# State-space stage: half-length folded frequency convolution, fused state products, and the sum of two planes on TensorE

## Chip, cores and metric

One core of a Trainium2 chip. The metric is the device time of one execution in microseconds, here the median of three runs.

## The reference, cut to what matters

Six blocks follow one another on x (8 sequences, 256 tokens, 128 channels): feed-forward, attention, feed-forward, mixture of experts, state-space, mixture of experts. The change is in the state-space block, and it prepares weights in the attention block.

```python
xz = einsum('bld,ed->bel', layernorm(x), in_proj_w)       # 512 rows: x and z, 256 channels each
out   = mamba_branch(xz, ...)                             # for each of 16 states: h = dA * h + dBu; y = sum(h * C)
out_b = mamba_branch(xz[:, :, ::-1], ...)                 # the same backwards, with weights of its own
x, z = split(xz, 2, axis=1)
xf = fftn(x, axes=(-2, -1))                               # over 256 channels and 256 tokens
xc = concatenate([xf.real, xf.imag], axis=1)              # 512 channels
xc = silu(conv(xc, fft_conv_w, width 5, padding 2) + fft_conv_b)
re, im = split(xc, 2, axis=1)
v = abs(ifftn(re + 1j * im, axes=(-2, -1)) * max(silu(z)))
y = out + out_b[:, :, ::-1] + normalized(v)
x = x + einsum('bdl,od->blo', y, out_proj_w)
```

All of it is f32. Since x is real, its transform is symmetric: the value at (-channel, -token) is the conjugate of that at (channel, token).

## The kernel before

Each block is a phase with its own tiles, semaphores and instruction streams, and a barrier stands between phases. `mamba_phase` (from L1349) runs its eight sequences in a pipeline written out by hand: `mamba_schedule` (L1315) calls `step(f, m, o)` of each engine, where f is the sequence whose inputs are made, m the one that is scanned, and o the one that is finished. A step has eight slots (UNITS), and each slot scans one unit of m: one direction and four of the 16 states, for two halves of 128 channels (DC = 2). All waits are semaphores, and every engine works its stream in order.

In a unit TensorE spreads four rows of B and of C over the partitions into PSUM (`spread`, L1524); ScalarE makes the decays (`decay`, L1678); VectorE multiplies B with dx for each half (L1811), scans each half (L1818) and multiplies each half with C (L1823); GpSimd adds four planes to two (L1940) and two to one (`halve`, L1943); TensorE sums that plane into y in PSUM (`total`, L1536), two slots later. h has three buffers (HBUFS), so VectorE's unit n waits for the sum of unit n - 3.

The frequency path of m runs beside that on TensorE in pieces: token transform (slot 0, L1469), ScalarE's copy (L1687), channel transform (L1478), ScalarE's copies into `fc` (L1691), the convolution over 4 input and 4 output blocks and 5 taps, 80 f32 products of 256 columns in slots 1 to 5 (L1489, PIECES), SiLU on ScalarE from PSUM (L1697, slot 5), and the inverse transforms in slots 6 and 7 (L1499, L1508). An f32 product is two records in the trace. In slot 6 `project_out` (L1561) follows these on TensorE, and VectorE's `add_output` (L1883) waits for it.

GpSimd also splits B and C into bf16 parts in slots 4 and 6 (`parts`, L1957 to L1963) and fetches the next sequence's input in slot 4 (`fetch`, L1949). VectorE ends a step with `steps` (L1784, L1789) and begins the next with `energy` (L1828); between the units lie small instructions for o (L1833, L1836, L1843, L1851, L1877).

In `attn_phase` (from L764) a step handles one sequence and four heads. There GpSimd rotates (L993, L995) and normalizes (L1002), and TensorE transposes what that leaves (L841). SP's queue is empty in that phase; the state-space weights (`cw`, 5 MB, among them) are loaded in the phase before the state-space one.

Of the kernel before, what the change touches and what calls it, by code (L numbers as in the profile page):

```python
# [763 lines left out]
def attn_phase(k, a):  # L764
# [3 lines left out]
    with ExitStack() as ctx:  # L768
# [11 lines left out]
        stx = k.sb("at_stx", [P, 2, 2, 6], ctx)  # L780
        sc = [k.psum(f"at_sc{h}", [P, 2, N], ctx) for h in range(4)]
# [4 lines left out]
                 "pr_sb", "rinv_sb", "pn01_sb", "pn23_sb", "tp_ps", "pt_sb", "cx_ps", "cx_sb", "op_ps", "x_sb"]  # L786
# [200 lines left out]
        def _(pool):  # L987
# [17 lines left out]

            for step in steps:
# [300 lines left out]

# [41 lines left out]
def mamba_phase(k, w):  # L1349
# [4 lines left out]
    winr, gw = w.winr, w.gm[:, 0, :, :]  # L1354
    dd = w.gm[:, 1, :, :].rearrange("p t n -> p (t n)")[:, 0:2 * DC * P].rearrange("p (r c n) -> p r c n", r=2, c=DC)
    with ExitStack() as ctx:
# [31 lines left out]
        f_bank = [k.psum(f"mb_f{i}", [P, 512], ctx) for i in range(2)]  # L1388
# [6 lines left out]
                 "b_ps", "c_ps", "da_sb", "dbu_sb", "scan_sb", "hc_sb", "half_sb", "hs_sb", "y_ps", "ym_sb", "dd_sb", "dd_ps",  # L1395
# [19 lines left out]
        def _(pe):  # L1415
# [44 lines left out]
            def frequency(m, slot, half):  # L1460
# [3 lines left out]
                if slot == 0 and half == 1:  # L1464
                    if m.b == 0:
                        pe.wait_ge(s["gw_sb"], 2)
# [15 lines left out]
                elif slot in (1, 2, 3, 4, 5) and (slot > 1 or half == 1):  # L1482
# [9 lines left out]
                    if slot == 5 and half:  # L1492
                        last.then_inc(s["f_ps"], 1)
# [603 lines left out]
```

## Time and profile before

| | us |
|---|---|
| median of 3 runs (2118.87 to 2120.63) | 2119.89 |
| the profiled execution | 2119.23 |
| its span, first to last instruction | 2117.40 |
| TensorE busy | 1961.0 (93%) |
| VectorE busy | 1683.6 (80%) |
| ScalarE busy | 1313.8 (62%) |
| GpSimd busy | 1170.4 (55%) |

The profile calls TensorE PE (PEld its weight loads), VectorE DVE, ScalarE ACT, GpSimd POOL and SyncE SP. The shares are means over six blocks, so windows are read by stage: attention lies at about 490 to 805 us, the state-space stage at about 1327 to 2047 us, its first scanned sequence from 1360 us. Busy time counts overlapping instructions of an engine once. "[1.60 <-PE ps_mb_w L1561]" behind a row means that its engine was idle for 1.60 us before it, until that instruction released it.

### The profile page before, as it was taken

Reading aid. Unit: us, or ns where it says so; the run is one execution under the profiler, and the core shown is the slowest. Engines: PE = TensorE matmul, PEld = TensorE weight load, DVE = VectorE, ACT = ScalarE, POOL = GpSimd, SP = SyncE. Lnnn points to the kernel's source line nnn. Section 1 sums busy time; section 2 is a strip of 40 time slices with the busy share of each in tenths; the row PEclk is TensorE's granted clock in tenths of the full one; section 3 lists DMA queues with packets and bytes.
Section 4 is the critical chain, followed back from the end, with each engine's and each line's share of the span. In section 5 each row is a group of like instructions: output and inputs, shape, how many; then the busy total and the mean of one; then the engine's idle time right before and its main releaser. Section 6 shows DMA issues by size and latency. Waiting matters only on the chain. (4 is left out here: it accounts for less than half of the span.)

```text
span 2117.4 us, 39266 instructions
## 1 busy us (share of the span) xinstructions
PE 1961.0 (93%) x14044; PEld 1440.9 (68%) x14044; DVE 1683.6 (80%) x2822; ACT 1313.8 (62%) x2591; POOL 1170.4 (55%) x1605
## 2 busy tenths in 40 slices
PE   6999999968999995999999869799999999999978
PEld 5677776646888873677777636587787777877745
DVE  5877777766888875777777766599999999999974
ACT  1566666644777772766666543558577576685543
POOL 2666666615667765666667503264755646646323
PEclk9999999988999996999999979899999999999989
DMA  4666666620000003665666423000000000000000
GB/s 136 159 158 158 159 159 158 149 65 1 2 1 2 2 1 94 156 163 155 162 155 161 124 69 140 1 1 1 1 1 1 1 1 1 1 1 1 1 16 21
DMA packets 147745, 144.86 MB, mean 68 GB/s; under 512 B 14048, under 2 KB 106976, under 8 KB 146912
## 3 DMA queue, kind: packets, MB, share of 16 engines
q1 hardware_dynamic: 127968, 132.91, 23.2%
q10 hardware_dynamic: 19584, 9.44, 2.5%
q8 instruction: 113, 1.85, 0.4%
q14 instruction: 80, 0.66, 0.1%
HBM read 94.07 MB, written 38.80 MB: 63 GB/s over the span
## 5 line engine op out<-in xcount | busy, mean ns | idle before, releaser
L577 DVE TENSOR_REDUCE sb_f_mx<-ps_f_s 128x2 f32<-128x512 f32 x768 | 501.9, 677 | 189.4 <-PE ps_f_s L354 186.3
L507 ACT ACTIVATE sb_f_pt<-ps_f_t 128x1024 f32<-128x1024 f32 x384 | 383.4, 1023 | 164.6 <-PE ps_f_t L371 162.4
L1940 POOL TENSOR_TENSOR sb_mb_h<-sb_mb_h 128x512 f32<-128x512 f32 x128 | 165.0, 1311 | 303.4 <-DVE sb_mb_h L1823 302.3
L354 PE MATMUL ps_f_s<-sb_f_stack 96*128 96x256 bf16 x1536 | 302.2, 279 | 27.8 <-DMA sb_f_stack<-f_scr 13.9
L1818 DVE TENSOR_TENSOR_SCAN sb_mb_h<-sb_mb_da,sb_mb_h 128x1024 f32<-128x1024 f32 x128 | 304.3, 2416 | 2.7 <-ACT sb_mb_da L1678 2.7
L1489 PE MATMUL ps_mb_f<-sb_mb_fc,sb_mb_cw 128*128 128x256 f32 x1280 | 286.8, 381 | 6.7 <-ACT sb_mb_fc L1691 6.6
L1489 PEld LDWEIGHTS ps_mb_f<-sb_mb_fc,sb_mb_cw 128*128 128x128 f32 x1280 | 239.7, 190 | 41.4 <-ACT sb_mb_fc L1691 8.9
L371 PE MATMUL ps_f_t<-sb_f_stack 128*128 128x256 bf16 x1536 | 232.1, 273 | 9.0 <-DMA sb_f_stack<-sb_f_mrow 5.3
L1678 ACT ACTIVATE sb_mb_da<-sb_mb_dl,sb_mb_an 128x255 f32<-128x255 f32 x512 | 211.0, 495 | 31.2 <-DVE sb_mb_h L1818 30.6
L354 PEld LDWEIGHTS ps_f_s<-sb_f_stack 96*128 96x128 bf16 x1536 | 131.8, 99 | 129.1 <-issue 44.0
L428 PE MATMUL ps_f_a<-sb_f_pt,sb_f_v 128*32 128x256 f32 x3072 | 189.1, 387 | 0.0
L371 PEld LDWEIGHTS ps_f_t<-sb_f_stack 128*128 128x128 bf16 x1536 | 146.5, 97 | 37.4 <-DMA sb_f_stack<-sb_f_mrow 12.4
L1811 DVE TENSOR_TENSOR sb_mb_h<-ps_mb_b,sb_mb_dx 128x1024 f32<-128x1024 f32 x128 | 149.9, 1210 | 10.3 <-PE ps_mb_b L1524 10.3
L1823 DVE TENSOR_TENSOR sb_mb_h<-sb_mb_h,ps_mb_c 128x1024 f32<-128x1024 f32 x128 | 148.6, 1200 | 1.6 <-PE ps_mb_c L1524 1.6
L1002 POOL TENSOR_SCALAR sb_at_pr<-sb_at_pr,sb_at_rinv 128x256 f32<-128x256 f32 x128 | 116.1, 927 | 60.8 <-DVE sb_at_rinv L925 60.8
L669 POOL TENSOR_SCALAR sb_f_nmx<-sb_f_mx 128x16 f32<-128x16 f32 x96 | 36.5, 380 | 188.8 <-DVE sb_f_mx L577 188.8
L428 PEld LDWEIGHTS ps_f_a<-sb_f_pt,sb_f_v 128*32 128x32 f32 x3072 | 91.3, 111 | 72.6 <-issue 24.5
L1042 ACT ACTIVATE sb_at_pr<-ps_at_sc,sb_at_nmx 128x256 f32<-128x256 f32 x256 | 118.9, 492 | 5.9 <-DVE sb_at_nmx L919 3.4
L1943 POOL TENSOR_TENSOR sb_mb_h<-sb_mb_h 128x256 f32<-128x256 f32 x128 | 118.6, 948 | 0.0
L690 POOL TENSOR_TENSOR sb_f_r<-sb_f_qf,sb_f_parts 128x512 f32<-128x512 f32 x96 | 113.9, 1186 | 7.7
L695 POOL TENSOR_TENSOR sb_f_parts<-sb_f_r,sb_f_parts 128x512 bf16<-128x512 f32 x96 | 111.7, 1163 | 7.7
L1027 ACT ACTIVATE sb_at_pt<-ps_at_tp 128x512 f32<-128x512 f32 x128 | 69.9, 604 | 66.0 <-PE ps_at_tp L841 66.0
(248 smaller groups left out, 3998.2 us busy)
## 6 DMA issues: line engine op xcount, KB each, us to landing
f_scr<-sb_f_parts SPq DMA_DIRECT2D x96, 384.0 KB, 2.8
sb_f_stack<-f_scr SPq DMA_DIRECT2D x192, 192.0 KB, 3.1
sb_f_stack<-f_scr SPq DMA_DIRECT2D x192, 128.0 KB, 3.2
sb_f_stack<-f_scr SPq DMA_DIRECT2D x192, 64.0 KB, 3.3
sb_f_stack<-sb_f_mrow ACTq DMA_DIRECT2D x96, 96.0 KB
sb_mb_cw<-in_cw SPq DMA_DIRECT2D x1, 5120.0 KB, 19.8
sb_prep_wn<-in_wn SPq DMA_DIRECT2D x6, 512.0 KB, 7.3
sb_m_w<-in_w SPq DMA_DIRECT2D x6, 256.0 KB, 3.3
```

What stands on the lines that cost most here:

```text
L354: last = nc.tensor.matmul(s_bank[j % 2][:, h, :], stack[0:ROWS, a.n % STACKS, 0, g * GROUP + pair * 2 + h, half * P:(half + 1) * P], stack ...
L371: last = nc.tensor.matmul(t_bank[i % 2][:, h, :], stack[:, e.n % STACKS, 1, g * GROUP + h, half * P:(half + 1) * P], stack[:, e.n % STACKS ...
L428: last = nc.tensor.matmul(act_bank[h * SLOT:(h + 1) * SLOT, g * N:(g + 1) * N], v[:, u.two, half, h * NG + g, :], pt[:, u.two, g, half, h, ...
L507: nc.scalar.activation(pt[:, e.two, g, half, :, :], t_bank[i % 2][:, :, :], ACT.Exp).then_inc(s["pt_sb"], 1)
L577: nc.vector.tensor_reduce(mx[:, a.two, half, head:head + 2], s_bank[j % 2][:, :, :], AX.X, ALU.max)\
L1042: last = nc.scalar.activation(pr[:, m.two, i, :], sc[h][:, i % 2, :], ACT.Exp, scale=scale, bias=nmx[:, m.two, i:i + 1], accum_out=rsum[:, ...
L1489: last = nc.tensor.matmul(f_bank[(1 + oc // 2) % 2][:, (oc % 2) * N:(oc % 2 + 1) * N], cw[:, ic, tap, oc * P:(oc + 1) * P], fc[:, ic, tap: ...
L1678: last = nc.scalar.activation(da[:, un % 2, c, i, 1:N], dl[:, m.parity, r, c, 1:N], ACT.Exp, scale=an[:, r, c, n:n + 1])
L1811: nc.vector.tensor_tensor(hb[:, c, :, :], b_bank[:, :, :], dx[:, m.parity, r, c:c + 1, :].broadcast_to([P, SG, N]), ALU.mult)\
L1818: nc.vector.tensor_tensor_scan(flat, da[:, un % 2, c, :, :].rearrange("p i n -> p (i n)"), flat, 0.0, ALU.mult, ALU.add).then_inc(s["scan_ ...
L1823: nc.vector.tensor_tensor(hb[:, c, :, :], hb[:, c, :, :], c_bank[:, :, :], ALU.mult).then_inc(s["hc_sb"], 1)
L1940: nc.gpsimd.tensor_tensor(hb[:, c, 0:2, :], hb[:, c, 0:2, :], hb[:, c, 2:4, :], ALU.add).then_inc(s["half_sb"], 1)
```

## The change

- The convolution is computed on half the tokens. The even and the odd part of the spectrum are kept (`even`, `odd`), GpSimd makes eight sums and differences of neighbours (`neighbours`, 2 x 128 to 131 elements each), and TensorE multiplies ten folded inputs (FOLDS) by ten folded weights: 10 x 2 x 4 f32 products of 128 to 131 columns, in slots 1 to 4. VectorE unfolds the two halves (`unfold`, two instructions, after the scans of unit 5), ScalarE's SiLU then works in place in SBUF at the start of slot 6 (`gate_frequency`).
- The folded weights are made in the attention phase: `cwa` and `cwb` are loaded (10 MB), GpSimd combines them (38 additions of 128x512), SP stores them to `cw_scr`, from where `cw` is loaded.
- Both channel halves go through one instruction for the product with B, and one for that with C; the scans stay two.
- GpSimd's second halving goes; TensorE sums two planes into y instead of one.
- The transforms before the convolution shrink to what the symmetry leaves; PIECES has seven pieces; some calls in TensorE's slots change places.

```diff
-PIECES = (0, 10, 19, 28, 37, 46, 54, 62, 71, 80)
+PIECES = (0, 11, 21, 32, 44, 57, 68, 80)
+FOLDS = ((658, 129, 0), (789, 128, 128), (264, 130, 0), ...
 attn_phase, SP
+            for i in range(2 * DC):
+                sp.dma_start(wa[:, p, c, :, :], d["cwa"][:, p, c, :, :]).then_inc(raw[i], 16)
+                sp.dma_start(wb[:, p, c, :, :], d["cwb"][:, p, c, :, :]).then_inc(raw[i], 16)
+            for a in range(1, len(FOLDS)):
+                sp.wait_ge(s["wfold_sb"], 2 * a)
+                sp.dma_start(d["cw"][:, a, :, :], wf[:, a, :, :]).then_inc(s["w_stored"], 16)
+            sp.wait_ge(s["w_stored"], 16 * len(FOLDS))
 attn_phase, GpSimd, after rotate(f, 1)
+                for i in range(joined(step), joined(step + 1)):
+                    combine(i)
 mamba_phase, TensorE: frequency
-                        last = nc.tensor.matmul(f_bank[(1 + oc // 2) % 2][:, (oc % 2) * N:(oc % 2 + 1) * N],
-                                                cw[:, ic, tap, oc * P:(oc + 1) * P], fc[:, ic, tap:tap + N],
+                        if a >= 2 and n == 0:
+                            pe.wait_ge(s["fold_sb"], m.b * (len(FOLDS) - 2) + a - 1)
+                        last = nc.tensor.matmul(f_both[:, oc // 2, oc % 2 * N + to:oc % 2 * N + to + cols],
+                                                cw[:, a, ic, oc * P:(oc + 1) * P], fold[:, ic, at:at + cols],
 total
-                last = nc.tensor.matmul(y_bank[:, c, ::1 - 2 * r], k.ident[:, :], h[:, n % HBUFS, c, 0, :],
+                for i in range(SG // 2):
+                    last = nc.tensor.matmul(y_bank[:, c, ::1 - 2 * r], k.ident[:, :], h[:, n % HBUFS, c, i, :],
 ScalarE
+            def gate_frequency(m):
+                act.wait_ge(s["split_sb"], m.b + 1)
+                for oc in range(XC_CH):
+                    last = nc.scalar.activation(fs[:, oc, :], fs[:, oc, :], ACT.Silu, bias=cb[:, oc:oc + 1])
 VectorE: scan
-                for c in range(DC):
-                    nc.vector.tensor_tensor(hb[:, c, :, :], b_bank[:, :, :],
-                                            dx[:, m.parity, r, c:c + 1, :].broadcast_to([P, SG, N]), ALU.mult)\
+                nc.vector.tensor_tensor(hb, both(b_bank), dx[:, m.parity, r, :, :].rearrange("p c (o n) -> p c o n", o=1)
+                                        .broadcast_to([P, DC, SG, N]), ALU.mult).then_inc(s["dbu_sb"], 1)
                 dve.wait_ge(s["da_sb"], n)
+                dve.wait_ge(s["dbu_sb"], n)
                 for c in range(DC):
...
+                if un == 5:
+                    unfold(m)
                 dve.wait_ge(s["c_ps"], n)
+                dve.wait_ge(s["scan_sb"], DC * n)
+                nc.vector.tensor_tensor(hb, hb, both(c_bank), ALU.mult).then_inc(s["hc_sb"], 1)
+            def unfold(m):
+                dve.wait_ge(s["f_sb"], FREQ * m.b + 4)
+                half = f_split[:, :, :, HALF_N - 1:0:-1]
+                nc.vector.tensor_tensor(fs4[:, :, :, 1:HALF_N], half, diff, ALU.add)
+                nc.vector.tensor_tensor(fs4[:, :, :, N - 1:HALF_N:-1], half, diff, ALU.subtract).then_inc(s["split_sb"], 1)
 GpSimd: halve, step
+                pool.wait_ge(s["hc_sb"], n)
                 for c in range(DC):
                     nc.gpsimd.tensor_tensor(hb[:, c, 0:2, :], hb[:, c, 0:2, :], hb[:, c, 2:4, :], ALU.add).then_inc(s["half_sb"], 1)
-                for c in range(DC):
-                    nc.gpsimd.tensor_tensor(hb[:, c, 0, :], hb[:, c, 0, :], hb[:, c, 1, :], ALU.add).then_inc(s["hs_sb"], 1)
+                    if m and un in (1, 2, 3):
+                        for a in range(3 * un - 1, min(3 * un + 2, len(FOLDS))):
+                            neighbours(m, a)
                     if m:
                         halve(m, un)
```

## Rows read from the trace of the kernel before

**Rows 1.** Windows; us, busy of PE, PEld, DVE, ACT, POOL, clock, DMA share, GB/s

```profile
600.00:700.00 100.00, 100.00 (x910) 81.14 (x904) 81.96 (x197) 75.19 (x241) 69.73 (x88) 1.00 0.01 2
1610.00:1690.00 80.00, 78.89 (x366) 61.75 (x366) 78.23 (x64) 54.15 (x108) 48.55 (x40) 1.00 0.00 1
1960.00:1970.00 10.00, 7.13 (x28) 5.35 (x28) 9.96 (x9) 7.57 (x15) 3.61 (x4) 0.83 0.01 2
```

**Rows 2.** Waits of DVE, 1449 to 1960 us: us in total, times, longest

```profile
DVE sb_x L1883 <- PE ps_mb_w L1561: 10.2, 6, 2.2
```

**Rows 3.** Timeline of DVE, one sequence: start us, us, engine line op

```profile
1713.06 0.67 DVE L1833 TENSOR_REDUCE sb_mb_zm<-sb_mb_sz 128x2 f32<-128x512 f32 x1
1713.77 0.84 DVE L1836 SCALAR_TENSOR_TENSOR sb_mb_zo<-sb_mb_zm 128x2 f32<-128x2 f32 x1
1714.53 2.34 DVE L1811 TENSOR_TENSOR sb_mb_h<-ps_mb_b,sb_mb_dx 128x1024 f32<-128x1024 f32 x2
1716.80 4.46 DVE L1818 TENSOR_TENSOR_SCAN sb_mb_h<-sb_mb_da,sb_mb_h 128x1024 f32<-128x1024 f32 x2
1721.18 2.32 DVE L1823 TENSOR_TENSOR sb_mb_h<-sb_mb_h,ps_mb_c 128x1024 f32<-128x1024 f32 x2
...
1724.08 0.67 DVE L1851 TENSOR_TENSOR sb_mb_ys<-ps_mb_y,sb_mb_sz 128x512 f32<-128x512 f32 x1
...
1736.23 4.70 DVE L1818 TENSOR_TENSOR_SCAN sb_mb_h<-sb_mb_da,sb_mb_h 128x1024 f32<-128x1024 f32 x2
...
1746.14 5.08 DVE L1818 TENSOR_TENSOR_SCAN sb_mb_h<-sb_mb_da,sb_mb_h 128x1024 f32<-128x1024 f32 x2
...
1755.65 5.05 DVE L1818 TENSOR_TENSOR_SCAN sb_mb_h<-sb_mb_da,sb_mb_h 128x1024 f32<-128x1024 f32 x2
...
1765.13 5.40 DVE L1818 TENSOR_TENSOR_SCAN sb_mb_h<-sb_mb_da,sb_mb_h 128x1024 f32<-128x1024 f32 x2
```

**Rows 4.** Timeline of POOL, the same sequence

```profile
1712.09 2.50 POOL L1940 TENSOR_TENSOR sb_mb_h<-sb_mb_h 128x512 f32<-128x512 f32 x2 [8.39 <-DVE sb_mb_h L1823]
1714.55 1.42 POOL L1943 TENSOR_TENSOR sb_mb_h<-sb_mb_h 128x256 f32<-128x256 f32 x2
...
1755.16 3.39 POOL L1943 TENSOR_TENSOR sb_mb_h<-sb_mb_h 128x256 f32<-128x256 f32 x2
```

**Rows 5.** Groups by line and form, PE: count, busy us, mean ns, idle before

```profile
L1489 PE MATMUL ps_mb_f<-sb_mb_fc,sb_mb_cw 128*128 128x256 f32 x1280 | 286.8, 381 | 6.7 <-ACT sb_mb_fc L1691 6.6
...
L1536 PE MATMUL ps_mb_y<-sb_mb_h,sb_ident 128*128 128x256 f32 x256 | 66.1, 381 | 3.3 <-POOL sb_mb_h L1943 3.3
...
L867 PE MATMUL ps_at_vc<-sb_at_wo,sb_at_cx 128*128 128x128 f32 x256 | 33.9, 275 | 0.7 <-ACT sb_at_cx L1034 0.7
...
L1478 PE MATMUL ps_mb_f<-sb_mb_yk,sb_mb_gm 128*128 128x256 f32 x128 | 30.9, 396 | 3.6 <-ACT sb_mb_yk L1687 3.6
```

**Rows 6.** Timeline of DVE, first scanned sequence, three waits

```profile
1374.66 4.47 DVE L1818 TENSOR_TENSOR_SCAN sb_mb_h<-sb_mb_da,sb_mb_h 128x1024 f32<-128x1024 f32 x2 [2.68 <-ACT sb_mb_da L1678]
...
1421.02 2.35 DVE L1823 TENSOR_TENSOR sb_mb_h<-sb_mb_h,ps_mb_c 128x1024 f32<-128x1024 f32 x2 [1.31 <-PE ps_mb_c L1524]
...
1435.68 2.35 DVE L1811 TENSOR_TENSOR sb_mb_h<-ps_mb_b,sb_mb_dx 128x1024 f32<-128x1024 f32 x2 [2.48 <-PE ps_mb_b L1524]
```

**Rows 7.** Timeline of ACT, the sequence of rows 3

```profile
1715.46 1.06 ACT L1691 ACTIVATE sb_mb_fc<-ps_mb_f 128x512 f32<-128x512 f32 x2
```

**Rows 8.** Timeline of POOL, attention, a middle step and the last

```profile
654.40 3.63 POOL L1002 TENSOR_SCALAR sb_at_pr<-sb_at_pr,sb_at_rinv 128x256 f32<-128x256 f32 x4 [1.72 <-DVE sb_at_rinv L925]
...
791.71 3.62 POOL L1002 TENSOR_SCALAR sb_at_pr<-sb_at_pr,sb_at_rinv 128x256 f32<-128x256 f32 x4 [5.10 <-DVE sb_at_rinv L925]
```

**Rows 9.** DMA issues: out<-in, queue, count, KB each, median us to landing

```profile
f_scr<-sb_f_parts SPq DMA_DIRECT2D x96, 384.0 KB, 2.8
```

**Rows 10.** Timeline, end of attention

```profile
802.67 0.42 DVE L944 TENSOR_TENSOR sb_x<-sb_x,ps_at_vc 128x256 f32<-128x256 f32 x1 [8.71 <-PE ps_at_vc L867]
```

**Rows 11.** One line's instructions, PEld: ns min/median/max, first and last start

```profile
L867 PEld LDWEIGHTS ps_at_vc<-sb_at_wo,sb_at_cx x256: 186/192/192, 518.8 to 802.2; 128*128 128x128 f32 x128
```

More of the change, by code:

```diff
@@ L1472, in frequency @@
                     pe.wait_ge(s["f_sb"], seen + 1)
[L1473 to L1482 removed]
+                    for part, cols in enumerate((slice(0, EVEN_COLS), slice(EVEN_COLS, EVEN_COLS + ODD_COLS))):
+                        n = cols.stop - cols.start
+                        for mc in range(DC):
+                            last = nc.tensor.matmul(f_bank[part][:, mc * n:(mc + 1) * n], gw[:, mc * P:(mc + 1) * P], yt[:, cols],
+                                                    start=True, stop=True)
+                        last.then_inc(s["f_ps"], 1)
+                elif slot in (1, 2, 3, 4) and (slot > 1 or half == 1):
                     piece = 2 * slot + half - 3
@@ L1502, in frequency @@
                         last.then_inc(s["f_ps"], 1)
-                elif slot == 7 and half == 1:
-                    pe.wait_ge(s["f_sb"], seen + 5)
-                    for dc in range(DC):
-                        for c in range(XC_CH):
-                            ri, kc = divmod(c, 2)
-                            last = nc.tensor.matmul(f_bank[(1 + dc) % 2][:, :],
-                                                    uk[:, kc, ri * CH_I + dc * P:ri * CH_I + (dc + 1) * P], gi[:, c, :],
-                                                    start=c == 0, stop=c == XC_CH - 1)
-                    last.then_inc(s["f_ps"], 1)
+                elif slot == 7:
+                    dc = half
+                    if dc == 0:
+                        pe.wait_ge(s["f_sb"], seen + 6)
+                    for c in range(XC_CH):
+                        ri, kc = divmod(c, 2)
+                        last = nc.tensor.matmul(f_bank[dc], uk[:, kc, ri * CH_I + dc * P:ri * CH_I + (dc + 1) * P], gi[:, c, :],
+                                                start=c == 0, stop=c == XC_CH - 1)
+                    if dc == 1:
+                        last.then_inc(s["f_ps"], 1)
             def spread(m, un, which):
@@ L1521, in spread @@
                     pe.wait_ge(s["bc_sb"], 2 * m.b + 2)
-                since(pe, read, DC * (m.b * UNITS + un))
+                since(pe, read, m.b * UNITS + un)
                 for i in range(SG):
@@ L1565, in combine @@
             def combine():
-                for part in range(2):
-                    cols = w.gm[:, :, 0:2, :] if part == 0 else w.gm[:, :, 2:3, :]
-                    for c in range(DC):
-                        last = nc.tensor.matmul(f_bank[part][:, 0:(2 - part) * CH_I], winr[:, c, :],
-                                                cols[:, c, :, :].rearrange("p t n -> p (t n)"), start=c == 0, stop=c == DC - 1)
+                for c in range(DC):
+                    last = nc.tensor.matmul(f_bank[0][:, 0:CH_I], winr[:, c, :], w.gm[:, c, :], start=c == 0, stop=c == DC - 1)
                 last.then_inc(s["gw_ps"], 1)
@@ L1721, in step @@
                 for slot in range(UNITS):
+                    if m and slot == 6:
+                        gate_frequency(m)
                     if f and 2 <= slot <= 6:
```

260 lines of the change are left out of this document (167 added, 93 removed).

## The prediction

> **What bounds the kernel now.** I read the windows by stage first. In the attention stage TensorE is busy 100 of 100 us, with VectorE at 82 and GpSimd at 70; in the state-space stage TensorE is busy 78.9 and VectorE 78.2 of 80 us [rows 1]. So the stage that the change rewrites has two full engines, and taking work from one of them is worth only what the other waits for it. The waits give that figure: in six whole sequences (1449 to 1960 us) VectorE waited 10.2 us, always in front of the same instruction, the output addition of L1883, which waits for TensorE: 1.7 us a sequence [rows 2]. With six sequences in 511 us, one takes about 85 us, and VectorE's own instructions are some 83 of it.
>
> The timeline of VectorE in one sequence shows of what they are made [rows 3]. A unit (there are eight) is two products with B, two scans, two products with C. In unit 1: products 1714.53 to 1716.80 (2.27 us), scans to 1721.18 (4.38), products of 2.32 us, of which 2.24 count, since the next instruction overlaps them. Instructions that don't need the one just before start some 0.07 us before it ends (1714.53 + 2.34 is 1716.87, the first scan, which needs only the first product, starts at 1716.80). One that needs it starts 0.04 us after its end (L1833 ends at 1713.06 + 0.67 = 1713.73, L1836 starts at 1713.77).
>
> A third thing is in these rows: the same two scans take 4.46 us in unit 1, but 4.70, 5.08, 5.05 and 5.40 in units 3 to 6, 2.39 us more in a sequence. GpSimd's timeline says why [rows 4]: the second halving takes 1.42 us for its two instructions when no scan runs, and 3.39 us in unit 5, where it meets the scans. VectorE instructions with two SBUF inputs and GpSimd get in each other's way. The products read PSUM and don't: the pair at 1714.53 and the second halving at 1714.55 ran side by side, with 2.34 and 1.42 us.
>
> **TensorE's part, costed from the rows by form [rows 5].** The convolution is 1280 records of 256 columns, 286.8 us, 224 ns each; the folded one has as many, of 128 to 131 columns. L867 has f32 records of 128 columns: 33.9 us for 256, 132 ns each. So 1280 x 132 = 169 us, 118 less. The channel transform (L1478) goes from 128 records of 256 columns to 64 of about 131: 30.9 to 8.4 us, 22 less. The sum into y gets 256 records more (L1536: 66.1 us for 256, of which I count all). Net 118 + 22 - 66 = 74 us, 9 us a sequence. None of that is on the path beyond the waits of [rows 2], and in the first sequence 1.31 and 2.48 us for TensorE and 2.68 us for ScalarE [rows 6], of which I give the change half, since the chain ahead of it gets a shorter set-up product. Of the 1.7 us I take back 1.1: the output projection still stands behind the eight wide products of slot 6, and these now wait for SiLU, which has been moved behind VectorE's unfolding; and TensorE will stand idle for some us before slot 6. Where it was idle for 2.9 of 10 us, the granted clock was 0.83 on average, part of it at the lower of its two levels (1.2 instead of 2.4 GHz) [rows 1]. The ends are 0 and 1.7.
>
> **VectorE's part, a sequence.** Fusing: one product of 2048 elements. 512 elements take 0.67 us (L1851), 1024 take 1.21 (two overlapped in 2.34), so 2048 take 2.29. The scan now needs the whole product just ahead of it: 2.29 + 0.04 against 2.27, +0.06. The second product needs the scan just ahead: 4.46 + 0.04 against 4.38, +0.12. The second product itself is 2.22 against 2.24. That is +0.16 a unit, 1.28 for eight, less 0.12 in unit 5, where the unfolding stands between: **+1.15**. (If a dependent start cost nothing, -0.55: the lower end. The upper is the sum.)
>
> Unfolding: two additions of 508 elements, one input in PSUM. L1851 has that size: 0.67 us, less the overlap of 0.07 [rows 3], twice: **+1.2**. No row reads PSUM backwards in VectorE; the slowest form here, the scan, takes about twice as long per element as a product, so 2.4 is the upper end, 1.2 the lower; I take the row of the same size.
>
> GpSimd against the scans: the second halving goes, but the first one now starts only when the whole fused product has ended (before, after its first half), runs 2.50 us [rows 4], and the next scan starts about 2.25 us after that end. So units 5 and 6 still meet it (0.25), and the B/C split (unit 4 and 6) and the fetch (unit 5) stay: I leave 0.6, 0.7 and 0.65 in units 4 to 6 and nothing in unit 3: 1.95 of the 2.39, -0.45. New are the eight neighbour additions of 258 elements with two SBUF inputs, in slots 1 to 3, each ahead of that slot's halving on GpSimd's queue. What waits behind them is the halving and, behind it, TensorE's sum, which VectorE needs only three units later; so the queue costs nothing, and the meeting with the scans does. The first three come when ScalarE has written the spectrum, which in this trace ends at 1715.46 + 1.06 = 1716.52 [rows 7], just ahead of the scans of unit 1 at 1716.80; the others follow the halvings of units 1 and 2. One instruction that gets between two scans costs about 0.5 (unit 5: 5.05 against 4.46), so 0.5 in each of three units and 0.25 for one that holds up the start in unit 2: 1.75. Together **+1.3**. Ends: -2.4 (no excess left and no meeting) and 8 x 0.59 - 0.45 = +4.3.
>
> Sum for a sequence: 1.15 + 1.2 + 1.3 - 1.1 = +2.55. Seven sequences so (the last counted like the six in the middle): +17.9. The first: 3.65 - 1.31 - 2.48 - 1.34 = -1.5.
>
> **Attention.** GpSimd gets 38 additions of 128x512, about 1.25 us each (the first halving has that size), one or two a step. Its free time ahead of L1002 is 1.72 us a step [rows 8], so one fits. Behind it on the queue stands L1002, whose result TensorE wants. Steps with two additions (five of 33) can stall TensorE for part of a microsecond: 0.8 in all. At the end five additions follow the last L1002 (791.71 + 3.62 = 795.33, so 801.6), then a store of 512 KB; one of 384 KB took 2.8 us [rows 9], so it lands at about 805, and VectorE's last addition of the stage ended at 803.1 [rows 10], with statistics behind it: 1.2. Together **+2**, ends 0 and 16 (0.5 in every step). The 10.5 MB loaded here and the 5 MB stored run on SP's queue, which has no other work in this stage; the first addition is due four steps in. The load of cw in the MoE stage has the size that it had.
>
> Sum: 17.9 - 1.5 + 2 = +18.4 on the profiled execution of 2119.2 us (span 2117.4), 2137.6; the median of the runs, 2119.9, lies 0.7 above it: **2138**.
>
> **A rule that says otherwise.** The rows show the 0.07 us overlap and the 0.04 us gap above [rows 3]. The Trainium skill (VectorE: DVE Perf Modes, "The DRAIN you can't avoid") says that the next instruction starts only when the pipe is empty, semaphore or not, and that fewer instructions is what counts. By that fusing would be the gain of rival 2; the rows speak against it.
>
> **Rivals.**
> 1. *GpSimd gets out of the way* (faster). The additions fall beside products, and with the second halving the excess goes: contention -2.4 instead of +1.3. A sequence is then 1.15 + 1.2 - 2.4 - 1.1 = -1.15, seven -8; the first -5.2; attention +2: **2109**. It decides once contention falls by more than 1.25 us a sequence. For it: the halving stands in the longest stretch of contention [rows 4]. Against it: scans are half of VectorE's time, and the B/C split stays.
> 2. *Dependent starts cost nothing*: fusing is then 2.29 - 0.07 = 2.22 us for each product in place of 2.27 and 2.24, -0.55 in eight units. A sequence +0.85, seven +6, the first -3.2, attention +2: **2125**.
> 3. *Weight loads bound the short products* (the change doesn't do what it says): the loads beside L867 last 192 ns [rows 11], and if the pace were 190 ns a record, the convolution would save 44 us and the transform 19, less than the 66 added. The waits for TensorE stay: eight sequences x 3.65 + 2 = +31: **2151**. L867's 132 ns speak against it.
> 4. *Attention pays*: 0.5 us in each of 33 steps, +16 instead of +2: **2152**. For it: TensorE is 100% busy there. Against it: 1.72 us of slack.
>
> **Chances.** Forecast 0.50 (its own range 2126 to 2150, from the ends of unfolding and contention taken in part), rival 1 0.18, rival 2 0.14, rival 3 0.06, rival 4 0.12. A measurement of this kernel can tell about 0.2% (4 us) from no change. Faster: rival 1 and the low end of rival 2, 0.20. The same: most of rival 2 and the low edge of the forecast, 0.14. Slower: the rest, 0.66. The range 2110 to 2152 leaves out half of rival 1 and the upper tails of 3 and 4.
>
> **What would show it.** Right: VectorE over 97% busy in the state-space stage and TensorE near 88%; a sequence of 87 us; records of the convolution near 132 ns; each scan pair of units 1 to 3 longer than 4.46 us; fused products near 2.29 us, the scan 0.04 us behind them. Wrong: scan pairs at 4.46 in units 1 to 3 (rival 1), no gap behind a product (rival 2), records near 190 ns (rival 3), TensorE under 98% in attention (rival 4).

## The result and the profile after

The changed kernel took 2141.74 us (median of four executions, 2137.34 to 2144.62), the kernel before 2120.26 beside it: a ratio of 1.0101, 95% interval 1.0082 to 1.0119. The profiled execution took 2142.74 us, its span is 2140.9, 23.5 us above the 2117.4 of before. Beside the experiments the kernel before had medians of 2115.2 to 2116.2, so kernels are compared below by their ratios, and by what one sequence takes in their traces. One execution of e6 below (2134.72 us, granted clock 0.91) was in a slower state of the chip and is left out of its ratio.

The windows by stage of the changed kernel (columns as in [rows 1]), and one whole sequence, from one output addition of VectorE to the next:

```profile
600.00:700.00 100.00, 99.55 (x900) 81.46 (x896) 83.91 (x197) 74.70 (x238) 83.88 (x99) 1.00 0.02 7
...
1610.00:1690.00 80.00, 68.01 (x378) 54.54 (x377) 78.37 (x49) 55.49 (x111) 37.48 (x29) 0.94 0.00 1
...
1785.50:1874.33 88.83, 75.50 (x409) 58.76 (x408) 85.39 (x53) 58.80 (x116) 44.27 (x34) 0.94 0.00 1
```

The same for a sequence of the kernel before:

```profile
1689.61:1774.37 84.76, 83.66 (x385) 64.94 (x384) 82.99 (x66) 58.44 (x112) 49.68 (x42) 1.00 0.00 1
```

TensorE lost 8 us of work in a sequence and the sequence grew by 4. The waits, first of VectorE and then of TensorE, in five sequences of the changed kernel (1520 to 1963 us), show who waits now:

```profile
DVE sb_x L1967 <- PE ps_mb_w L1627: 6.9, 6, 1.6
...
PE ps_mb_c L1588 <- DVE sb_mb_h L1900: 53.8, 28, 4.3
```

TensorE waits 53.8 us for VectorE, while VectorE's old wait, the one of [rows 2], is still there. VectorE's timeline of one sequence answers to [rows 3]; the numbering of the units is the same (unit 0 starts at 1800.25):

```profile
1800.25 2.28 DVE L1888 TENSOR_TENSOR sb_mb_h<-ps_mb_b,sb_mb_dx 128x2048 f32<-128x2048 f32 x1
1802.63 4.47 DVE L1894 TENSOR_TENSOR_SCAN sb_mb_h<-sb_mb_da,sb_mb_h 128x1024 f32<-128x1024 f32 x2
1807.21 2.29 DVE L1900 TENSOR_TENSOR sb_mb_h<-sb_mb_h,ps_mb_c 128x2048 f32<-128x2048 f32 x1
...
1813.17 5.27 DVE L1894 TENSOR_TENSOR_SCAN sb_mb_h<-sb_mb_da,sb_mb_h 128x1024 f32<-128x1024 f32 x2
...
1824.52 4.96 DVE L1894 TENSOR_TENSOR_SCAN sb_mb_h<-sb_mb_da,sb_mb_h 128x1024 f32<-128x1024 f32 x2
...
1831.98 1.25 DVE L1953 SCALAR_TENSOR_TENSOR sb_mb_nm<-sb_mb_mv,sb_mb_rs 128x2 f32<-128x2 f32 x1
...
1835.54 4.47 DVE L1894 TENSOR_TENSOR_SCAN sb_mb_h<-sb_mb_da,sb_mb_h 128x1024 f32<-128x1024 f32 x2
...
1859.68 0.66 DVE L1906 TENSOR_TENSOR sb_mb_yk<-ps_mb_f,sb_mb_fold 128x508 f32<-128x508 f32 x1
1860.26 0.67 DVE L1907 TENSOR_TENSOR sb_mb_yk<-ps_mb_f,sb_mb_fold 128x508 f32<-128x508 f32 x1
1860.85 2.27 DVE L1900 TENSOR_TENSOR sb_mb_h<-sb_mb_h,ps_mb_c 128x2048 f32<-128x2048 f32 x1
...
1865.42 5.05 DVE L1894 TENSOR_TENSOR_SCAN sb_mb_h<-sb_mb_da,sb_mb_h 128x1024 f32<-128x1024 f32 x2
```

Three things are to be seen. A scan starts 0.10 us after the end of the product that it needs (1800.25 + 2.28 = 1802.53, next start 1802.63), the product with C 0.11 us after the scans. Scan pairs of 4.47 us stand beside pairs of up to 5.27. And L1953, a product of two elements a partition, takes 1.25 us. GpSimd's timeline at the places of the last two and at the end of slot 5, which answers to [rows 4]:

```profile
1813.12 5.74 POOL L2053 TENSOR_TENSOR sb_mb_fold<-sb_mb_fold 128x260 f32<-128x260 f32 x3 [1.03 <-ACT sb_mb_fold L1757]
...
1831.95 2.51 POOL L2027 TENSOR_TENSOR sb_mb_h<-sb_mb_h 128x512 f32<-128x512 f32 x2 [6.80 <-DVE sb_mb_h L1900]
...
1863.20 2.50 POOL L2027 TENSOR_TENSOR sb_mb_h<-sb_mb_h 128x512 f32<-128x512 f32 x2 [5.59 <-DVE sb_mb_h L1900]
1865.66 2.67 POOL L2068 TENSOR_TENSOR sb_mb_bcf<-sb_mb_bcf,sb_mb_bc 128x256 f32<-128x256 f32 x1
```

The neighbour additions meet the scans at 1813.17. The halving that starts at 1831.95 holds the tiny product at 1831.98. The halving at 1863.20 starts when the whole fused product has ended and still runs when the next scans start, at 1865.42; the first addition of the B/C split (L2068) stands behind it and takes 2.67 us beside them.

TensorE at the end of slot 5 and in slot 6, where VectorE's wait comes from:

```profile
1863.18 1.03 PE L1588 MATMUL ps_mb_c<-sb_mb_bc,sb_mb_sel 128*128 128x256 bf16 x4 [4.28 <-DVE sb_mb_h L1900]
1864.00 5.52 PE L1562 MATMUL ps_mb_f<-sb_mb_gi,sb_mb_yk 128*128 128x512 f32 x8
...
1869.80 3.60 PE L1562 MATMUL ps_mb_f<-sb_mb_gi,sb_mb_yk 128*128 128x512 f32 x8
1873.23 1.05 PE L1627 MATMUL ps_mb_w<-sb_mb_wop,sb_mb_ys 128*128 128x128 f32 x8
```

After 4.28 idle us the first eight wide records take 5.52 us, the next eight 3.60. The projection stands behind all of them. The windows there have granted clocks of 0.80 and 0.86, so part of either is at the lower level, 1.2 GHz:

```profile
1855.00:1865.00 10.00, 5.72 (x27) 4.13 (x26) 10.00 (x6) 6.32 (x13) 4.41 (x4) 0.80 0.00 1
1865.00:1875.00 10.00, 10.00 (x33) 5.27 (x32) 8.33 (x6) 4.56 (x11) 8.65 (x7) 0.86 0.00 0
```

The groups of the new records, to be read beside [rows 5]:

```profile
L1601 PE MATMUL ps_mb_y<-sb_mb_h,sb_ident 128*128 128x256 f32 x512 | 133.8, 409 | 6.5 <-POOL sb_mb_h L2027 6.5
...
L1551 PE MATMUL ps_mb_f<-sb_mb_fold,sb_mb_cw 128*128 128x129 f32 x512 | 63.8, 279 | 0.1
```

The four forms of L1551 have 160.2 us for 1280 records, 125 ns each, with 192 ns weight loads beside them.

In attention, VectorE's last addition and the first instruction of the next block that waits for the barrier; first the changed kernel, then the kernel before, whose first row is in [rows 10]:

```profile
802.74 0.42 DVE L989 TENSOR_TENSOR sb_x<-sb_x,ps_at_vc 128x256 f32<-128x256 f32 x1 [7.11 <-PE ps_at_vc L912]
...
808.87 0.25 DVE L92 RECIPROCAL sb_rs<-sb_sd 128x16 f32<-128x16 f32 x1 [4.97 <-ACT sb_sd L86]
```

```profile
806.70 0.25 DVE L92 RECIPROCAL sb_rs<-sb_sd 128x16 f32<-128x16 f32 x1 [2.88 <-ACT sb_sd L86]
```

The added 23.5 us lie here: up to the first product with B 2.5 (1362.51 against 1360.03); from there to the first output addition, over two sequences, -2.4 (157.63 against 160.05); five middle sequences +19.1 (88.58 each, against 84.77); the rest to the last output addition +4.0; behind it +0.3.

### The profile page after: what moved, and what is told of

It is laid out like the page before. It is cut to its first block and busy times, and to the rows that moved or that the text cites. A ratio compares the mean times of both kernels' runs of the same rounds, so it can differ in the third digit from the quotient of the medians.

```text
span 2140.9 us, 39573 instructions
## 1 busy us (share of the span) xinstructions
PE 1894.6 (88%) x14232; PEld 1396.3 (65%) x14232; DVE 1709.5 (80%) x2713; ACT 1317.7 (62%) x2622; POOL 1180.8 (55%) x1579
## 5 line engine op out<-in xcount | busy, mean ns | idle before, releaser
L2027 POOL TENSOR_TENSOR sb_mb_h<-sb_mb_h 128x512 f32<-128x512 f32 x128 | 173.3, 1375 | 345.0 <-DVE sb_mb_h L1900 345.0
L371 PE MATMUL ps_f_t<-sb_f_stack 128*128 128x256 bf16 x1536 | 232.0, 273 | 11.5 <-DMA sb_f_stack<-sb_f_mrow 7.7
L1888 DVE TENSOR_TENSOR sb_mb_h<-ps_mb_b,sb_mb_dx 128x2048 f32<-128x2048 f32 x64 | 145.8, 2278 | 7.2 <-PE ps_mb_b L1588 7.2
L1900 DVE TENSOR_TENSOR sb_mb_h<-sb_mb_h,ps_mb_c 128x2048 f32<-128x2048 f32 x64 | 146.3, 2286 | 5.8
L1551 PE MATMUL ps_mb_f<-sb_mb_fold,sb_mb_cw 128*128 128x129 f32 (+3 forms) x1280 | 149.9, 276 | 1.2 <-POOL sb_mb_fold L2053 1.1
L1551 PEld LDWEIGHTS ps_mb_f<-sb_mb_fold,sb_mb_cw 128*128 128x128 f32 x1280 | 147.0, 193 | 2.0 <-POOL sb_mb_fold L2053 1.2
L1601 PE MATMUL ps_mb_y<-sb_mb_h,sb_ident 128*128 128x256 f32 x512 | 133.8, 409 | 6.5 <-POOL sb_mb_h L2027 6.5
L1601 PEld LDWEIGHTS ps_mb_y<-sb_mb_h,sb_ident 128*128 128x128 f32 x512 | 100.7, 206 | 26.1 <-POOL sb_mb_h L2027 8.7
```

What stands on the lines that cost most here:

```text
L371: last = nc.tensor.matmul(t_bank[i % 2][:, h, :], stack[:, e.n % STACKS, 1, g * GROUP + h, half * P:(half + 1) * P], stack[:, e.n % STACKS ...
L1551: last = nc.tensor.matmul(f_both[:, oc // 2, oc % 2 * N + to:oc % 2 * N + to + cols], cw[:, a, ic, oc * P:(oc + 1) * P], fold[:, ic, at:at ...
L1601: last = nc.tensor.matmul(y_bank[:, c, ::1 - 2 * r], k.ident[:, :], h[:, n % HBUFS, c, i, :], start=un == 0 and c == 0 and i == 0, stop=un ...
L1888: nc.vector.tensor_tensor(hb, both(b_bank), dx[:, m.parity, r, :, :].rearrange("p c (o n) -> p c o n", o=1) .broadcast_to([P, DC, SG, N]), ...
L1900: nc.vector.tensor_tensor(hb, hb, both(c_bank), ALU.mult).then_inc(s["hc_sb"], 1)
L2027: nc.gpsimd.tensor_tensor(hb[:, c, 0:2, :], hb[:, c, 0:2, :], hb[:, c, 2:4, :], ALU.add).then_inc(s["half_sb"], 1)
```

## The experiments

The table has every kernel. "Period" is a fifth of the time between the starts of two output additions five sequences apart. "Work" is the time of VectorE's instructions in it, each counted from its start to the start of the next, so that overlaps and small gaps are in it; what is left is waits. "Scans" is the scans' part of the work. Without contention the scans take 8 x 4.38 = 35.0 us where the product with C starts half by half (the overlap makes 4.38 of 4.46), and 36.5 to 36.6 where it needs both scans; what lies above is called their excess. The rest of the work is products with B and C (36.12 before, 36.76 changed, 36.23 in e1), unfolding (1.17 where there is one) and small instructions (9.53, 10.32 and 8.79). Each trace is of one execution, and those of e3, e4 and e6 are of their shortest or second shortest (2123.18 us where the median is 2132.40, 2128.79 where it is 2132.32, 2095.43 where it is 2108.25): the gains that their periods show are larger than those of their ratios. The diffs are shortened: the waits that change with an edit are left out, but for GpSimd's in e1.

| kernel | ratio to before, 95% | period | work | waits | scans |
|---|---|---|---|---|---|
| before | 1 | 84.77 | 83.10 | 1.67 | 37.45 |
| changed | 1.0101 (1.0082 to 1.0119) | 88.58 | 87.28 | 1.30 | 39.03 |
| e1, products per half | 1.0008 (0.9998 to 1.0018) | 85.32 | 82.17 | 3.15 | 35.98 |
| e2, output first | 1.0099 (1.0084 to 1.0114) | 87.56 | 86.77 | 0.79 | 38.65 |
| e3, no neighbours | 1.0078 (1.0065 to 1.0090) | 86.88 | 86.00 | 0.88 | 37.77 |
| e4, tiny instructions | 1.0068 (1.0056 to 1.0079) | 86.80 | 85.93 | 0.87 | 39.33 |
| e5 = e1 + e2 + e4 | 0.9964 (0.9952 to 0.9976) | 84.11 | 81.30 | 2.81 | 35.96 |
| e6 = e5, unfolding early | 0.9948 (0.9927 to 0.9969) | 82.15 | 81.17 | 0.98 | 35.89 |
| e7, only B fused | 1.0018 (1.0007 to 1.0030) | 85.47 | 83.23 | 2.24 | 36.40 |
| e8, before + fused products | 1.0109 (1.0093 to 1.0125) | 87.47 | 87.47 | 0.00 | 39.91 |
| e9, before + e2 + e4 | 1.0004 (0.9991 to 1.0018) | 85.08 | 82.30 | 2.78 | 37.30 |
| e10 = e1 + second halving | 1.0072 (1.0054 to 1.0089) | 86.86 | 86.05 | 0.81 | 39.17 |

**e1: products per half.**

```diff
-                nc.vector.tensor_tensor(hb, both(b_bank), dx[...both halves...], ALU.mult).then_inc(s["dbu_sb"], 1)
+                for c in range(DC):
+                    nc.vector.tensor_tensor(hb[:, c], b_bank, dx[...half c...], ALU.mult).then_inc(s["dbu_sb"], 1)
-                nc.vector.tensor_tensor(hb, hb, both(c_bank), ALU.mult).then_inc(s["hc_sb"], 1)
+                for c in range(DC):
+                    dve.wait_ge(s["scan_sb"], DC * (n - 1) + c + 1)
+                    nc.vector.tensor_tensor(hb[:, c], hb[:, c], c_bank, ALU.mult).then_inc(s["hc_sb"], 1)
 GpSimd: halve
-                pool.wait_ge(s["hc_sb"], n)
                 for c in range(DC):
+                    pool.wait_ge(s["hc_sb"], DC * (n - 1) + c + 1)
```

> Changed kernel with both products split per channel half again (32 instructions a sequence in place of 16, the waits counted per half), everything else as in the changed kernel. Theory: what fusing costs is the dependent start; an instruction that needs the one just ahead starts 0.10 us after its end, one that doesn't starts 0.07 us before it. A unit without contention then goes from 9.17 to 8.89 us, 2.1 us a sequence, eight sequences 17 us: 2125 us, a sequence near 86.5 in place of 88.6. Rival A (the size in the prediction, a gap of 0.04): 1.15 a sequence, 2132 us. Rival B (a dependent start costs nothing, fewer instructions win): 0.55 a sequence the other way, 2146 us.

The gain is larger than the theory's: work falls by 5.1 us, and 1.9 us of that come back as waits. VectorE's groups in five sequences of e1, and the same two of the changed kernel:

```profile
L1896 DVE TENSOR_TENSOR_SCAN sb_mb_h<-sb_mb_da,sb_mb_h 128x1024 f32<-128x1024 f32 x80 | 183.1, 2328 | 4.5 <-ACT sb_mb_da L1739 4.5
...
L1956 DVE SCALAR_TENSOR_TENSOR sb_mb_nm<-sb_mb_mv,sb_mb_rs 128x2 f32<-128x2 f32 x5 | 0.8, 160 | 0.2
```

```profile
L1894 DVE TENSOR_TENSOR_SCAN sb_mb_h<-sb_mb_da,sb_mb_h 128x1024 f32<-128x1024 f32 x80 | 191.9, 2439 | 4.1
...
L1953 DVE SCALAR_TENSOR_TENSOR sb_mb_nm<-sb_mb_mv,sb_mb_rs 128x2 f32<-128x2 f32 x5 | 6.3, 1258 | 0.2
```

The dependent starts are the part foreseen: products 36.76 to 36.23, and 1.42 in the scans (36.46 without contention, where the unfolding parts unit 5, to 35.04); 1.95 together. The other 3.2 are meetings with GpSimd: the scans' excess goes from 2.57 to 0.94, and all small instructions together from 10.32 to 8.79, of which L1953 has 1.10. The halving starts half a product earlier when the product with C comes in halves, and is done before the next scans, as GpSimd's and VectorE's timelines of e1 show:

```profile
1812.63 2.51 POOL L2030 TENSOR_TENSOR sb_mb_h<-sb_mb_h 128x512 f32<-128x512 f32 x2 [6.05 <-DVE sb_mb_h L1903]
...
1841.71 2.49 POOL L2030 TENSOR_TENSOR sb_mb_h<-sb_mb_h 128x512 f32<-128x512 f32 x2 [7.17 <-DVE sb_mb_h L1903]
1844.16 0.67 POOL L2071 TENSOR_TENSOR sb_mb_bcf<-sb_mb_bcf,sb_mb_bc 128x256 f32<-128x256 f32 x1
```

```profile
1806.98 4.46 DVE L1896 TENSOR_TENSOR_SCAN sb_mb_h<-sb_mb_da,sb_mb_h 128x1024 f32<-128x1024 f32 x2
...
1813.79 0.16 DVE L1956 SCALAR_TENSOR_TENSOR sb_mb_nm<-sb_mb_mv,sb_mb_rs 128x2 f32<-128x2 f32 x1
...
1844.95 4.82 DVE L1896 TENSOR_TENSOR_SCAN sb_mb_h<-sb_mb_da,sb_mb_h 128x1024 f32<-128x1024 f32 x2
```

What stands behind the halving on GpSimd's queue moves with it: in unit 6 the split's first addition (L2071) ends before the scans and takes 0.67 us instead of 2.67, and in unit 2 the neighbour additions end before the scans, whose pair takes 4.46 instead of 4.96. So part of what the neighbour additions cost (e3 below) is in these 3.2 too, and the two figures don't add up.

**e7: only the product with B fused.** In the changed kernel, e1's second edit alone:

```diff
-                nc.vector.tensor_tensor(hb, hb, both(c_bank), ALU.mult).then_inc(s["hc_sb"], 1)
+                for c in range(DC):
+                    nc.vector.tensor_tensor(hb[:, c], hb[:, c], c_bank, ALU.mult).then_inc(s["hc_sb"], 1)
```

> Changed kernel with only the product with C split per channel half again; the product with B stays one instruction of 2048 elements. Theory: the fused product with B costs its dependent start alone (0.1 us a unit, 0.9 a sequence), the fused product with C costs its own dependent start and moves GpSimd's halving half a product later, into the next scans: VectorE's own work in a sequence is then 83.1 us (82.2 in the fully split kernel, 87.3 in the changed one), and the scans' excess over 4.47 stays under 0.15 a unit. Rival: either fused product brings the contention: 85 us of VectorE's work, scans above 4.7 on average. In time: about 2123 against 2134.

The theory's 83.1 is met (83.23), the rival's 85 is not. The fused product with B costs its dependent start and a little contention: the scans' excess is 36.40 - 35.04 = 1.36 us, 0.17 a unit where under 0.15 was expected, and 0.4 above e1's 0.94. The rest of the scans' 1.6, and the small instructions' 1.5, belong to the fused product with C. By the page "VectorE: DVE Perf Modes" of the Trainium skill (section "Rules for kernel authors"), in a chain of VectorE instructions it is their number that is to be kept low, not that of the semaphores; here eight fewer cost 0.76 us (products with B 18.19 and 18.95), and the measurement decides.

**e8: fused products in the kernel before.** The opposite of e1's edits, made to the kernel before:

```diff
-                for c in range(DC):
-                    nc.vector.tensor_tensor(hb[:, c], b_bank, dx[...half c...], ALU.mult).then_inc(s["dbu_sb"], 1)
+                nc.vector.tensor_tensor(hb, both(b_bank), dx[...both halves...], ALU.mult).then_inc(s["dbu_sb"], 1)
-                for c in range(DC):
-                    nc.vector.tensor_tensor(hb[:, c], hb[:, c], c_bank, ALU.mult).then_inc(s["hc_sb"], 1)
+                nc.vector.tensor_tensor(hb, hb, both(c_bank), ALU.mult).then_inc(s["hc_sb"], 1)
```

> Kernel before with both products fused over the channel halves, nothing else of the change. Theory: dependent starts cost 2.0 us a sequence there too, and both halvings now start after the whole product with C, the second one in the scans of every unit: the scans' excess goes from 2.4 to about 5 us a sequence; against this the wait of 1.6 us for the output projection goes: a sequence of 89 us, 30 us above the kernel before. Rival: the cost is the dependent start alone, 2.0 less the wait of 1.6: a sequence of 85.2 us, 3 us above.

One part of the change alone makes the kernel before 1.09% slower, as much as the whole change. The size per sequence was overestimated (87.47, not 89): the scans' excess went from 2.4 to 3.3, not to 5. No wait was left on VectorE. Fused products and the second halving bring the same tiny stall as in the changed kernel:

```profile
L1869 DVE SCALAR_TENSOR_TENSOR sb_mb_nm<-sb_mb_mv,sb_mb_rs 128x2 f32<-128x2 f32 x5 | 6.3, 1257 | 0.2
```

**e10: the second halving back.** e1, and in `halve` and `total`:

```diff
+                for c in range(DC):
+                    pool.wait_ge(s["half_sb"], DC * (n - 1) + c + 1)
+                    nc.gpsimd.tensor_tensor(hb[:, c, 0, :], hb[:, c, 0, :], hb[:, c, 1, :], ALU.add).then_inc(s["hs_sb"], 1)
-                    for i in range(SG // 2):
-                        last = nc.tensor.matmul(y_bank[:, c, ::1 - 2 * r], k.ident[:, :], h[:, n % HBUFS, c, i, :],
+                    last = nc.tensor.matmul(y_bank[:, c, ::1 - 2 * r], k.ident[:, :], h[:, n % HBUFS, c, 0, :],
```

> Kernel with the products per channel half (the first run), with GpSimd's second halving back and one plane summed on TensorE in place of two; so the folded convolution and its unfolding are all that is left of the change. Theory: TensorE's 8 us a sequence are worth nothing, and the second halving meets the scans again: their excess over 4.38 a pair goes from 0.9 to about 3 us a sequence (2.4 in the kernel before, and the neighbour additions), a sequence from 85.3 to 86.5 us, 10 us more. Rival: the excess does not change, since the neighbour additions are few beside the first halving, and the shorter queue on TensorE cuts the wait for the output projection (2.3 us) instead: 84.5 us, 6 us less.

The theory's period of 86.5 was nearly met (86.86), with an excess of 39.17 - 35.04 = 4.1 where about 3 was expected. So moving the second halving to TensorE is worth 1.5 us a sequence, 3.9 of work less the waits that it lets appear. What is left of the change in e10 (the folding with its unfolding and neighbour additions, the shortened transforms, the weights made in attention) costs: 1.0072, though TensorE is busy for only 70.4 us a sequence (73.8 in e1, 83.7 before).

**e3: no neighbour additions** after the first sequence, so that the convolution multiplies the first sequence's sums; TensorE's waits for them are changed to match.

```diff
-                    if m and un in (1, 2, 3):
+                    if m and m.b == 0 and un in (1, 2, 3):
                         for a in range(3 * un - 1, min(3 * un + 2, len(FOLDS))):
                             neighbours(m, a)
```

> Changed kernel without GpSimd's neighbour additions in sequences 2 to 8; the convolution then multiplies the first sequence's sums, so part of the computation is left out. Theory: the additions meet VectorE's instructions with two SBUF inputs: the scans of units 2 and 3 fall from about 5.27 and 4.96 to 4.6 and the two-element product of L1953 from 1.18 to 0.2, 2.1 us a sequence, seven times: 2127 us. Rival: what remains of GpSimd's work (halving, split of B and C) makes the contention, the additions make none: 2141 us.

Half right. The scans lose 39.03 - 37.77 = 1.26 us, but L1953 keeps its time; what held it is the halving, as GpSimd's timeline above shows:

```profile
L1955 DVE SCALAR_TENSOR_TENSOR sb_mb_nm<-sb_mb_mv,sb_mb_rs 128x2 f32<-128x2 f32 x5 | 6.3, 1259 | 0.2
```

In time the ratio, 1.0078, lies between the theory's (2127 to 2120, 1.003) and the rival's (2141, 1.010), nearer to the rival's.

**e4: tiny instructions.**

```diff
-                nc.vector.scalar_tensor_tensor(zo, zm, -1.0, zm, ALU.mult, ALU.max)
-                nc.vector.scalar_tensor_tensor(nm, mv[:, :, 0], -1.0, rs, ALU.mult, ALU.mult)
+                for c in range(DC):
+                    nc.vector.tensor_scalar(nm[:, c:c + 1], mv[:, c, 0:1], rs[:, c:c + 1], -1.0, ALU.mult, ALU.mult)
-                        last = nc.scalar.activation(vv[:, c, :], vv[:, c, :], ACT.Copy, scale=zo[:, c:c + 1])
+                        last = nc.scalar.activation(vv[:, c, :], vv[:, c, :], ACT.Abs, scale=zm[:, c:c + 1])
```

> Changed kernel in which the two-element product L1953 is two instructions with one streamed input each, and the two-element L1920 is left out, its absolute value taken by ScalarE in the scaling that follows. Theory: an instruction with two SBUF inputs, however small, waits for GpSimd's running one; with one input it does not: L1953 from 1.18 to about 0.2 us for both, L1920's 0.66 gone, 1.6 us a sequence, seven times: 2130 us. Rival: any small VectorE instruction waits for GpSimd: 0.66 a sequence, 2137 us; or the scan that follows meets the same GpSimd work and gives it back: 2141 us.

```profile
L1952 DVE TENSOR_SCALAR sb_mb_nm<-sb_mb_mv,sb_mb_rs 128x1 f32<-128x1 f32 x10 | 1.7, 209 | 0.2
```

The theory's mechanism held: 209 ns an instruction where the form with two streamed inputs took 1258 (it starts at 1821.13 in that trace, a halving at 1821.10). The scans got 0.30 us worse and the wait 0.43 shorter, so that the period fell by 1.8; the ratio, 1.0068, lies between the theory's (2130, 1.005) and the first rival's (2137, 1.008). The Trainium skill ("SBUF — State Buffer", "Who interferes with whom") says that VectorE's second read port is the one GpSimd uses, and its first its own; the rows agree.

**e2: output projection first**, in TensorE's `step`.

```diff
+                    if o and slot == OUT_SLOT:
+                        project_out(o, f, m)
                     if m:
                         frequency(m, slot, 0)
...
                         frequency(m, slot, 2 if slot == 0 else 1)
-                    if o and slot == OUT_SLOT:
-                        project_out(o, f, m)
```

> Changed kernel with the output projection put ahead of slot 6's inverse transforms in TensorE's order, nothing else. Theory: VectorE's output addition waits 1.3 us a sequence only because the projection stands behind sixteen wide records, the first eight of them at the lower clock; the wait goes to under 0.2, seven times: 2133 us. Rival: the inverse transforms and the spread of B behind them come 1 us later and VectorE waits for those instead (a product with B that waits for its spread), 2141 us.

The wait for the projection went to nothing and another came, the first scan's for ScalarE's decays:

```profile
DVE sb_mb_h L1894 <- ACT sb_mb_da L1739: 4.0, 4, 1.7
```

The period falls by 1.0 us instead of 1.3; in the ratio that can't be told from the changed kernel.

**e5 and e6: the edits together, then the unfolding between the two scans of unit 5.**

```diff
                     nc.vector.tensor_tensor_scan(flat, ...)
-                if un == 5:
-                    unfold(m)
+                    if un == 5 and c == 0:
+                        unfold(m)
```

> Changed kernel with the three edits of the earlier runs together: products per channel half, output projection ahead of slot 6's inverse transforms, the two-element instructions without a second SBUF input. Theory: the unfused kernel's sequence of 85.3 us loses its 2.3 us wait for the output projection and 0.7 us of two-element work, and keeps a wait of 0.9 us of the scans for ScalarE's decays: 82.4 us against 84.8 of the kernel before, seven or eight times: 17 to 19 us below the kernel before. Rival: VectorE gives the time back as a longer wait for the decays, since ScalarE's SiLU stands behind VectorE's unfolding: a sequence of 84 us, 5 us below the kernel before.

> The kernel of the three edits, with the unfolding between the two scans of unit 5 in place of behind both. Theory: ScalarE's SiLU starts 2.2 us earlier, the decays behind it too, and the scan's wait for them (0.9 us) goes; the unfolding itself costs the same: a sequence of 81.6 us, 6 us below the kernel of the three edits. Rival: the wait for the decays comes from elsewhere (they wait for the scans two units back), and nothing changes.

In e5 the rival held (84.11): ScalarE is late, since its SiLU waits for VectorE's unfolding. VectorE's waits in five sequences of e5, then of e6:

```profile
DVE sb_mb_h L1896 <- ACT sb_mb_da L1739: 8.2, 5, 1.7
DVE sb_mb_vv L1915 <- ACT sb_mb_uk L1773: 5.5, 5, 1.8
```

```profile
DVE sb_mb_h L1896 <- ACT sb_mb_da L1739: 4.6, 5, 1.6
```

Unfolding one scan earlier takes 2 us off the period in the traces; a wait of 0.9 for the decays stays, so 82.15 and not 81.6. In time that gain isn't shown: the medians of e5 and e6 are 2108.35 and 2108.25, and the intervals of their ratios overlap. Both kernels are faster than the two given ones, by 0.4 and 0.5% against the kernel before. For e6 its period would give about 8 x 2.6 = 21 us, 1%. Its other executions differ, and with their mean granted clock: 2094 to 2105 us at 0.954 to 0.959, 2108 to 2113 at 0.950 to 0.952. Which stage loses it in the longer ones isn't known, since the one profile is of a short one (2095.43).

**e9: what the folding is for.** The kernel before with the edits of e2 and e4.

> Kernel before (old convolution, products per channel half, both halvings) with two edits of the later runs: output projection ahead of slot 6's inverse transforms, two-element instructions without a second SBUF input. Theory: VectorE's own work falls from 83.1 to about 82.5 us a sequence, but TensorE's 83.7 us of busy time in a sequence of 84.8 then bounds it: 83.9 us a sequence, 7 us below the kernel before; the folded convolution is worth what lies below that (82.2 us with the early unfolding). Rival: TensorE's order gives VectorE what it needs in time all the same, and a sequence takes 82.6 us, 17 us below; the folded convolution is then worth nothing even there.

```profile
DVE sb_mb_h L1811 <- PE ps_mb_b L1524: 13.9, 5, 3.3
```

VectorE's work fell to 82.30 and the period stayed: the wait moved to the product with B, 2.8 us a sequence, for TensorE, which is busy 83.9 of 85.1 us. The theory's bound was right and its 83.9 too good. Without the folding, and in this order of TensorE's work, TensorE ends the matter; with it, e5 and e6 get to 84.11 and 82.15, and to ratios of 0.9964 and 0.9948 where e9 has 1.0004. So the freed time is worth something only once VectorE's own work has come below it.

## Why the prediction was right

The sign and the size (2138, measured 2141.74 and 2142.74 profiled) came out; the terms of the sum did so in part, and the size is in part luck: in the largest error, contention, two mistakes cancelled. Of the signs named, attention and the records of the convolution came out; VectorE is busy for 96% of a sequence (85.39 of 88.83 us) where over 97 was named, and TensorE for 85% where 88 was.

- *TensorE's freed time is worth only the waits*: right. The freed time itself is 78 us (286.8 - 160.2 in the convolution, 30.9 - 11.5 in the channel transform, less 133.8 - 66.1 for the sum) where 74 was worked out; records of 125 ns rule out rival 3. Part of it goes back to the lower clock: the same 128 records of 512 columns take 56.3 us before (L1499) and 69.6 here (L1562).
- *1.1 of 1.7 us of wait taken back*: 0.4 (1.67 to 1.30), a term sized too large. The causes named, the eight wide products, the SiLU behind the unfolding and the lower clock, are what the rows show; they weigh more.
- *Fusing, +1.15 a sequence*: dependent starts cost 1.95. The gap of 0.04 was read from two small instructions; behind these long ones it is 0.10 to 0.11, in sixteen places of a sequence. The lost overlap of 0.07 was in the sum. Rival 2 is out: e7 shows a fused product slower. The section of the Trainium skill that the prediction quotes ("VectorE: DVE Perf Modes", "The DRAIN you can't avoid") itself adds that an instruction that isn't held starts earlier; the overlap of 0.07 us agrees with that.
- *Unfolding, +1.2*: 1.17 (L1906 and L1907, start to start).
- *Contention, +1.3*: the step that failed. Against the kernel before the scans have +0.16 and the small instructions +0.79 (10.32 against 9.53), so the net, 0.95, looks right. But the second halving's going was given 0.45, where e10 against e1 shows 3.2 in the scans, and the fused product's later halving was let meet "units 5 and 6" for 0.25, where e1 shows 3.2 a sequence, in scans and in small instructions that the prediction didn't price (L1953), in part from what stands behind the halving on GpSimd's queue. The neighbour additions cost 1.26 (e3), not 1.75. Two errors of about 3 us cancelled, by luck. The sign named for the units held in 1 and 2 (5.27, 4.96) and not in 3 (4.47).
- *Rival 1* is what the change does without the fused products: an excess of 0.94 in e1, 1.5 below the kernel before, and 0.7 less in the small instructions, where the rival had 2.4. It was held for a rival to the whole, and is a part with the opposite sign.
- *A sequence*: 3.81 instead of 2.55. *The first*: the first two sequences together were to bring -1.5 + 2.55 = +1.05 and brought -2.4. VectorE's waits in them fell from 9.6 to 1.0 us, 8.6 where 6.2 was counted: of ScalarE's 2.68 in [rows 6], counted half, nothing is left. Its work rose by 6.2.
- *Attention, +2*: TensorE waits for softmax five times, 3.3 us, against once, 1.8, in the kernel before (waits of TensorE, 500 to 800 us): 1.5 where 0.8 was foreseen. The four new waits, of 0.20 to 0.45 us, come 4 to 5 us behind the four pairs of additions that fall in one step. From the last addition to L92 it takes 2.1 us more (6.13 against 4.03) where the store was given 1.2; in the other eight kernels with the new stage it takes only 0.4 to 0.8 more (4.43 to 4.84). From the stage's first L951 (L906 before) to L92 the nine kernels with the new attention stage take 324.7 to 328.4 us, the three with the old one 321.9 to 324.0: 4.1 more in the mean and 2.8 between the two given kernels, so the term of 2 was too small. Rival 4's 16 us are out; TensorE is 99.55% busy. No run took the preparation out by itself.

## What to carry to other kernels

Fusing two instructions saved nothing here, where the engine runs them back to back with overlap, and it cost what was started after the first of them: look at who waits for the first half (here GpSimd's halving), at what stands behind that on its queue, and at what this work then collides with. An engine's freed time is worth what another engine waits for it, until the other's own work is cut below it; so cut first on the engine that is full, then free its partner. A net term that comes out right can hide two wrong ones; undo each part by itself, in the kernel before too.

## What was not expected

- A VectorE instruction of two elements a partition takes 1258 ns instead of 160 when it has two SBUF inputs and starts just behind the start of a halving, as long as one of the halving's two additions (1.25 us); in e4, with one streamed input, 209. In e1 it starts 1.16 us behind the halving's start (1813.79 against 1812.63) and takes 0.16, so the rows read as if it ended with the addition that is running. [rows 3] had it already: L1836, also of two elements, took 0.84 us and ended at 1714.61, where the halving of [rows 4] ended at 1714.59.
- A dependent start costs 0.17 to 0.18 us on VectorE behind these products and scans (2.3 and 4.5 us): 0.10 to 0.11 behind the end of the instruction needed, and the 0.07 of overlap.
- The kernels with less work on TensorE have a lower clock: in whole sequences the granted clock is 1.00 before and in e8 and e9, 0.94 in the changed kernel, 0.93 in e10, where TensorE is idle most. The first records behind 4.28 idle us took half again as long (5.52 against 3.60).
